# A selective scan with a mixture of experts: the states' sum over n moved from VectorE into TensorE's transposes

## The reference

```python
def step(state, inp):
    ut, dtt, bt, ct = inp
    dA = jnp.exp(jnp.clip(dtt[:, :, None] * A, -5.0, 5.0))
    dB = dtt[:, :, None] * bt[:, None, :] * ut[:, :, None]
    state = dA * state + dB + 1e-06
    y = jnp.sum(state * ct[:, None, :], axis=-1) + D * ut
    return (state, y)
```

## Time and profile before

| | us |
|---|---|
| median of 3 runs | 1398.56 (1398.08 to 1398.73) |
| profiled execution, span | 1397.1 |
| busy: TensorE / VectorE / ScalarE / GpSimd | 1212.7 / 1174.3 / 916.8 / 846.8 |
| weight loads on TensorE, beside its matmuls | 1013.2 |

### The profile page before, as it was taken

How to read it: one execution, slowest core, us unless ns; L and a number is a source line. 1 busy time by engine, 2 the same in 40 slices (tenths; PEclk the granted TensorE clock), 3 DMA queues, 4 the chain that set the end, 5 groups by cost and what they waited for, 6 DMA issues and landing times.

```text
span 1397.1 us, 27129 instructions
## 1 busy us (share of the span) xinstructions
PE 1212.7 (87%) x8709; PEld 1013.2 (73%) x8709; DVE 1174.3 (84%) x2236; ACT 916.8 (66%) x1464; POOL 846.8 (61%) x1370
## 2 busy tenths in 40 slices
PE   6878897899989898998989899898989989898883
PEld 4556666577877777777777778777877878787773
DVE  1699999998898979998898989989798988998423
ACT  4665666577875766777676777668577768772321
POOL 4445445854366864768656783768647684665554
PEclk9899999999999999999999999999999999999997
DMA  6000000032322343143321433232330333256783
GB/s 179 1 1 9 1 9 6 22 125 61 114 82 64 106 136 103 44 128 99 121 67 34 147 97 98 86 111 81 109 120 29 125 92 121 78 184 190 251 271 85
DMA packets 111646, 132.29 MB, mean 95 GB/s; under 512 B 10128, under 2 KB 82704, under 8 KB 111504
## 3 DMA queue, kind: packets, MB, share of 16 engines
q1 hardware_dynamic: 98416, 111.31, 25.7%
q0 software_dynamic: 8192, 16.79, 4.0%
q10 hardware_dynamic: 4896, 2.43, 0.6%
HBM read 102.37 MB, written 28.11 MB: 93 GB/s over the span
## 4 chain that ended last, share of the span: by engine, by line
PE 35%; DVE 31%; ACT 13%; issue 12%; POOL 5%; DMA 2%; DVEq 0%; POOLq 0%; SPq 0%; ACTq 0%
DVE h L1281 14%; DVE yT L1299 11%; PE p_db L1036 5%; PE p_misc L1060 5%; PE p_hT L1053 5%; PE p_dn L1218 4%; PE p_gu L1206 3%; ACT dA L872 3%; ACT L969 2%; POOL ysel L791 2%; ACT hm L969 2%; PE p_gu L1197 2%; PE p_misc L1097 2%; PE p_misc L1141 1%; PE p_misc L1115 1%
## 5 line engine op out<-in xcount | busy, mean ns | idle before, releaser
L1281 DVE TENSOR_TENSOR_SCAN h<-dA,p_db 128x512 f32<-128x512 f32 x512 | 602.4, 1205 | 86.3 <-PE p_db L1036 85.3
L735 POOL TENSOR_SCALAR dBT<-wT,bcT 128x256 f32<-128x256 f32 x704 | 337.1, 479 | 249.2 <-ACT wT L903 140.1
L1299 DVE SCALAR_TENSOR_TENSOR yT<-p_hT,bcT,yT 128x256 f32<-128x256 f32 x960 | 402.2, 472 | 18.0 <-PE p_hT L1053 17.9
L872 ACT ACTIVATE dA<-dt_sb,A_sb 128x510 f32<-128x510 f32 x512 | 330.6, 710 | 26.6 <-DVE h L1281 25.5
L1036 PE MATMUL p_db<-ident,dBT 128*128 128x128 f32 x2048 | 284.4, 277 | 49.4 <-DVE h L1281 44.0
L1053 PE MATMUL p_hT<-ident,h 128*128 128x128 f32 x2048 | 288.9, 279 | 29.8 <-DVE yT L1299 16.6
L1036 PEld LDWEIGHTS p_db<-ident,dBT 128*128 128x128 f32 x2048 | 233.4, 142 | 96.7 <-issue 84.7
L1053 PEld LDWEIGHTS p_hT<-ident,h 128*128 128x128 f32 x2048 | 233.0, 143 | 74.8 <-issue 42.2
L777 POOL DMA_INDIRECT xs_dram<-xn,slot x128 | 127.0, 992 | 90.0 <-ACT dA L872 38.3
L929 ACT ACTIVATE dBT<-wT,eps,bcT 128x256 f32<-128x256 f32 x320 | 163.9, 593 | 0.0
L791 POOL DMA_INDIRECT ysel<-ys_dram,slot x128 | 123.5, 965 | 57.0 <-issue 33.9
(11 more groups left out here) (189 smaller groups left out, 1533.1 us busy)
## 6 DMA issues: line engine op xcount, KB each, us to landing
wring<-w_moe_dram SPq DMA_DIRECT2D x169, 384.0 KB, 4.3
xt<-xs_dram SPq DMA_DIRECT2D x41, 256.0 KB, 5.7
ys_dram<-yo SPq DMA_DIRECT2D x34, 256.0 KB, 2.3
dA<-w_moe_dram SPq DMA_DIRECT2D x16, 384.0 KB, 5.6
x_sb<-x_dram SPq DMA_DIRECT2D x16, 256.0 KB, 4.5
out_dram<-x SPq DMA_DIRECT2D x15, 256.0 KB, 2.5
xs_dram<-ysel SPq DMA_DIRECT2D x4, 512.0 KB, 6.0
xs_dram<-xn,slot POOLq DMA_INDIRECT x128, 2.3
```

The source lines that it names most:

```text
L735: op = pool.tensor_scalar(dBT[:, j % DBT_RING, c], wT[:, g % 2, c], bcT[:, g % 2, c, n:n + 1], STATE_EPS, ALU.mult, ALU.add)
L872: act.activation(dst[:, :, 1:], src[:, :, 1:], ACT.Exp, scale=A_sb[:, half, n:n + 1]).then_inc(exp_done, 1)
L1281: dve.tensor_tensor_scan(h[:, j % 2, half], dA[:, j % DA_RING, half], p_db[half][:], 0.0, ALU.mult, ALU.add).then_inc(scan_done, 1)
L1299: op = dve.scalar_tensor_tensor(yT[:, g % 2, cc], p_hT[pair][:, c], bcT[:, g % 2, cc, NS + n:NS + n + 1], yT[:, g % 2, cc], ALU.mult, ALU.add)
```

## The change

- The scan writes its result over its own input in the PSUM bank p_db. A second VectorE instruction for each half ("t0", "t1") multiplies the bank by C and writes h in SBUF, 128x512. h has three buffers, dA five.
- With channels on partitions, C is a row over tokens, the same in all partitions. So C is transposed once a group ("cT"), copied to c_rows, stored to DRAM by SP ("cs"), and for each unit SP loads its row of 512 numbers spread over all 128 partitions into c_wide ("c", a ring of six, three units ahead).
- TensorE's transposes of h ("h") accumulate over the 16 units of a group in the PSUM pair p_y. VectorE's 60 sums and ScalarE's 4 products a group go. ScalarE copies p_y to yT once a group ("e0", "e1"), and the first unit of the next group waits for that copy.
- A half of p_db is free again when its product with C has ended.
- The orders of all engines are new. DVE_SLOTS, PE_SLOTS and SP_SLOTS are shown; those of ScalarE and GpSimd, and the tables for start and end, are new too. At the end c_wide also holds experts' weights.

```diff
-BY_ACT = 1
-
 COMB_DVE = 4
-DA_RING = 6
+DA_RING = 5
+H_RING = 3
+C_RING = 6
+C_LEAD = 3
 DBT_RING = 3
 DB_LEAD = 2
...
 PE_SLOTS = (
-    "U h N G i0 i1 X", "h U yb0 N i0 i1 yb1 G", "X h U xnT i0 i1 N G", "h u0 N U v0 i0 i1 X X",
-    "N h U G op i0 i1", "U X G h u1 v1 G N i0 i1 h", "U X xn2T G i0 i1 dt0 f0 X",
-    "N h dt1 f1 N U i0 i1 logit X G", "h N U i0 i1 G bc N X", "h U i0 i1", "h G G N X U z0 i0 i1 z1",
-    "h X N U G i0 i1 X U rank", "N h i0 i1", "h G X wT0 U N wT1 G i0 i1 h X N X", "U G N i0 i1 h G",
-    "U i0 i1 X")
+    "h U N yb0 G i0 U i1 h", "N G i0 X G i1 U G U", "yb1 U i0 N h G X xnT h", "i1 u0 i0 N X v0 N i1 op",
+    "i0 h X i1 N u1 G N i0", "X h i1 U U v1 h i0 X", "xn2T G i1 dt0 X f0 h U i0", "dt1 N f1 i1 h logit i0 G N",
+    "X i1 U U i0 X bc N i1", "h G h X i0 G i1 z0 G", "U N N G i0 z1 U cT i1", "U N i0 X G X h rank N",
+    "i1 h X wT0 U i0 wT1 i1 N", "G h G U i0 i1 N h X", "G U X X i0 h i1")
 DVE_SLOTS = (
-    "stats1 s0 s1 y0 P y1", "C Q s0 s1 Q P yd0 y0", "s0 s1 yd1 y1 Q C y0 y1", "s0 C C y0 s1 P y1 P Q",
-    "s0 s1 P y0 y1 x1 C", "stats2 s0 s1 C y0 Q Q P y1", "s0 s1 y0 P y1", "s0 y0 s1 C Q y1 s0 lg P Q",
-    "s1 Q C y0 P C", "s0 y1 s1 r y0 r y1 r P r r s0 r", "Q C s1 r y0 y1 r P r Q r s0 s1 r",
-    "r y0 r P y1 r C C Q r", "s0 r s1 r y0 y1 r r", "C P r r s0 s1 Q r y0 y1 r Q r",
-    "r r C s0 P s1 r r y0 r P y1", "s0 C s1 C Q y0 Q P y1")
+    "C stats1 Q s0 s1 t0 t1 P s0 s1", "Q Q t0 t1 yd0 Q s0 t0 Q s1", "P yd1 P t1 P s0 t0 P s1 t1",
+    "s0 t0 C s1 t1 C x1 C C Q", "s0 t0 s1 C Q stats2 C P t1 s0", "s1 C t0 t1 s0 C t0 P s1 t1",
+    "s0 P t0 s1 t1 lg s0 r t0 s1", "C Q r P r t1 Q s0 Q r", "t0 r s1 Q r C P t1 r s0", "P r r t0 r s1 r t1 s0 r",
+    "P C t0 r C s1 r P r t1", "r s0 r r Q r r r t0 r", "P s1 r t1 Q r s0 r C r", "s1 t0 t1 C P r Q s0 s1 r",
+    "t0 t1 P C r Q Q")
...
 SP_SLOTS = (
-    "", "Y T W W xl Y W", "T", "Y O Y W T", "O W T O O", "T Y T Y W W", "", "Y Y T W T T", "",
-    "T O O O O Y W W", "", "Y Y W O W T T O O W", "", "Y Y W O", "Y T T W W", "T O O Y Y O O T")
+    "W c c O W O", "W Y W W T c", "c T W Y W O", "c Y c O T Y", "T T c Y c c", "O xl W T Y O", "c T Y Y T Y",
+    "T W c O c T", "W W O Y T Y", "W cs c T T O", "O T O Y c Y", "W W O O Y Y", "W c W Y T T", "O O O c")
...
-        h = sb("h", [P, 2, HALVES, TOK])
-        yT = sb("yT", [P, 2, CHUNKS, CH])
-        y_more = sb("y_more", [P, CHUNKS, CH]) if BY_ACT > 1 else None
+        h = sb("h", [P, H_RING, HALVES, TOK])
+        c_wide = sb("c_wide", [P, C_RING, TOK])
+        yT = sb("yT", [P, CHUNKS, CH])
...
-        p_hT = [pb(f"p_hT{i}", [P, 2, CH]) for i in range(PAIRS)]
+        p_y = [pb(f"p_y{i}", [P, 2, CH]) for i in range(PAIRS)]
...
+            def store_rows(g):
+
+                sp.wait_ge(misc_emptied, misc_at["cT", g])
+                at_least(sp, times_c, HALVES * NS * (g - 1))
+                sp.dma_start(row_sets[g % 2].rearrange("n (c t) -> c n t", c=CHUNKS), c_rows[:]).then_inc(rows_stored, 16)
+
+            def load_c(j):
+                if not 0 <= j < UNITS:
+                    return
+
+                g, n = divmod(j, NS)
+                if n == 0:
+                    sp.wait_ge(rows_stored, 16 * (g + 1))
+                at_least(sp, times_c, HALVES * (j - C_RING + 1))
+                sp.dma_start(c_wide[:, j % C_RING], row_sets[g % 2][n:n + 1].broadcast_to([P, TOK])
+                             ).then_inc(c_loaded[j % C_RING], 16)
+
...
+                if name == "cT":
+
+                    at_least(act, rows_stored, 16 * g)
+                    act.activation(c_rows[:], bank[0:CHUNKS * NS, 0:P], ACT.Copy).then_inc(misc_emptied, 1)
...
-            def multiply_state(g, n, pair):
-
-                if g is None:
-                    return
-                j = NS * g + n
-                act.wait_ge(hT_in_psum, PAIRS * j + pair + 1)
-                if n == pair == 0:
-                    act.wait_ge(misc_emptied, misc_at["bc", g])
-                    if g >= 2:
-                        act.wait_ge(misc_in_psum, misc_at["yb1", g - 2])
-                at = (BY_ACT - 1) * g + n - 1
-                if n:
-                    at_least(act, more_added, PAIRS * (at - 1) + pair + 1)
-                for c in range(2):
-                    cc = 2 * pair + c
-                    into = yT[:, g % 2, cc] if n == 0 else y_more[:, cc]
-                    op = act.activation(into, p_hT[pair][:, c], ACT.Copy, scale=bcT[:, g % 2, cc, NS + n:NS + n + 1])
-                op.then_inc(mul_done, 1)
+            def empty_y(g, pair):
+
+                act.wait_ge(y_in_psum, PAIRS * (NS * g + NS - 1) + pair + 1)
+                if pair == 0:
+                    at_least(act, misc_in_psum, misc_at["yb1", g - 1] if g else 0)
+                act.activation(yT[:, 2 * pair:2 * pair + 2], p_y[pair][:], ACT.Copy).then_inc(y_emptied, 1)
...
-                at_least(pe, scan_done, 2 * (j - 1) + half + 1)
+                at_least(pe, times_c, 2 * (j - 1) + half + 1)
...
-            def states_by_token(j):
+            def sum_states(j):
                 if not 0 <= j < UNITS:
                     return
 
-                pe.wait_ge(scan_done, 2 * j + 2)
+                g, n = divmod(j, NS)
+                pe.wait_ge(times_c, HALVES * (j + 1))
                 for pair in range(PAIRS):
-                    if j and (j - 1) % NS < BY_ACT:
-                        pe.wait_ge(mul_done, sums_before(j - 1, pair, True))
-                    elif j:
-                        pe.wait_ge(mac_done, sums_before(j - 1, pair, False))
+                    if n == 0:
+                        at_least(pe, y_emptied, PAIRS * (g - 1) + pair + 1)
                     for c in range(2):
                         for half in range(HALVES):
                             t0 = (2 * pair + c) * P
-                            mm = pe.transpose(p_hT[pair][:, c, half * P:(half + 1) * P],
-                                              h[:, j % 2, half, t0:t0 + P], ident[:])
-                    mm.then_inc(hT_in_psum, 1)
+                            mm = pe.matmul(p_y[pair][:, c, half * P:(half + 1) * P],
+                                           h[:, j % H_RING, half, t0:t0 + P], ident[:], is_transpose=True,
+                                           start=n == c == half == 0, stop=n == NS - 1 and c == half == 1,
+                                           skip_group_check=True)
+                    mm.then_inc(y_in_psum, 1)
...
-                    pe.wait_ge(mac_done, sums_before(NS * g + NS - 1, 1, False))
+                    pe.wait_ge(y_emptied, PAIRS * (g + 1))
                     for c in range(CHUNKS):
                         mm = pe.transpose(bank[:, c * P:(c + 1) * P],
-                                          yT[:, g % 2, c, half * P:(half + 1) * P], ident[:])
+                                          yT[:, c, half * P:(half + 1) * P], ident[:])
...
-                    at_least(dve, hT_in_psum, PAIRS * (j - 1))
                     dve.wait_ge(clamp_done, j + 1)
                 dve.wait_ge(db_by_pe, 2 * j + half + 1)
-                dve.tensor_tensor_scan(h[:, j % 2, half], dA[:, j % DA_RING, half], p_db[half][:], 0.0,
+                dve.tensor_tensor_scan(p_db[half][:], dA[:, j % DA_RING, half], p_db[half][:], 0.0,
                                        ALU.mult, ALU.add).then_inc(scan_done, 1)
 
-            def sum_states(j, pair):
+            def multiply_states(j, half):
                 if not 0 <= j < UNITS:
                     return
 
-                g, n = divmod(j, NS)
-                if n < BY_ACT:
-                    return
-                dve.wait_ge(hT_in_psum, PAIRS * j + pair + 1)
-                if n == BY_ACT == 1:
-                    dve.wait_ge(mul_done, sums_before(j - 1, pair, True))
-                elif n == BY_ACT:
-                    dve.wait_ge(more_added, PAIRS * ((BY_ACT - 1) * (g + 1) - 1) + pair + 1)
-                at_least(dve, mac_done, sums_before(j - 1, pair, False))
-                for c in range(2):
-                    cc = 2 * pair + c
-                    op = dve.scalar_tensor_tensor(yT[:, g % 2, cc], p_hT[pair][:, c],
-                                                  bcT[:, g % 2, cc, NS + n:NS + n + 1],
-                                                  yT[:, g % 2, cc], ALU.mult, ALU.add)
-                op.then_inc(mac_done, 1)
+                dve.wait_ge(scan_done, HALVES * j + half + 1)
+                if half == 0:
+                    at_least(dve, y_in_psum, PAIRS * (j - H_RING + 1))
+                    dve.wait_ge(c_loaded[j % C_RING], 16 * (j // C_RING + 1))
+                dve.tensor_tensor(h[:, j % H_RING, half], p_db[half][:], c_wide[:, j % C_RING], ALU.mult
+                                  ).then_inc(times_c, 1)
```

## The result

The changed kernel takes 1337.03 us (median of 4 runs, 1329.57 to 1340.43), the kernel before 1398.64 in the same rounds: ratio 0.9546, 95% interval 0.9515 to 0.9576. It is 61.6 us faster where 44.6 were forecast. The profiled execution has a span of 1333.1 us, against 1397.1 before.

The account below looks back on a forecast made before the run. TensorE and VectorE, neither full, wait for each other in turns; -3.3 (products) - 0.9 (p_hT) + 1.2 (p_db) = -3.0 us a group, times 15.6 = 46.8, plus 2.5 at the ends: 1354 us, range 1318 to 1410.

Parts of the forecast that it names:

- waits at p_hT: VectorE's wait for the transposes into p_hT, 0.9 us a group, goes.
- Products: VectorE's 32 products with C cost 21.9 us a group, replacing 25.2 of products and sums: a gain of 3.3.
- The scan in PSUM: VectorE's scan writing PSUM instead of SBUF: change taken as 0, up to 0.13 us either way; dearer-scan rival, chance 0.10.
- The handover of p_db: p_db is released only after the product, so VectorE's wait there grows from 5.0 to 6.2 us a group.
- The slower rival: Late p_db refills put scan, product and refill in one ring: +2.5 us a group, 1440 us in all; chance 0.20.
- What TensorE gains: TensorE's 1.6 us a group of waits at p_hT go; summing in PSUM costs nothing; transposing C adds some 0.2.
- larger-gain rival: TensorE's waits at p_misc go too, or PSUM scans are cheaper: 75.6 us a group, 1323 us; chance 0.17.
- C's rows: Loads of C's rows arrive in time, cost nothing; rival: one bare 5 us wait a group, 1432 us, chance 0.05.
- Start and end: First product's store and load cost 2 us at the start; last sums' products, transposes and copies add 0.5 at the end.
- 15.6 equal periods: The 1257 us from first scan to last sums count as 15.6 group periods, each gaining 3.0 us: 46.8 us.

Follow-up runs that it names:

- one_sbuf_input: Changed kernel, but the scan writes its own SBUF buffer and the product multiplies that by p_db, not C's row: ratio 0.956 (1378.7 us, slower chip).
- refills_together: Changed kernel, with TensorE's refill of p_db's half 1 moved right behind that of half 0: 1502.3 us on a slower chip, ratio 1.043.
- no_c_loads: Changed kernel with C's rows loaded only for the first six units, later units reusing them: 1333.0 us, ratio 0.954.
- old_end: Changed kernel with the five tables for the end as in the kernel before, p_y's two copies put ahead on ScalarE: 1324.5 us, ratio 0.947.
- half_product: Changed kernel with only 256 of a half's 512 columns multiplied by C's row: 1309.0 us, ratio 0.936.
- half_turns: Changed kernel with half 1's transposes of h made only in the first unit of a group: 1312.5 us, ratio 0.939.

## Why the prediction was right, and where it wasn't

The direction and the range held; the time was 17 us too high. The closeness is partly luck. The forecast for a group was -3.0 us, and in the even part it is -6.8, more than twice that; what keeps the whole near the forecast is that only ten groups gained so much and the end lost. On VectorE's side the forecast was -3.3 (products), -0.9 (waits at p_hT) and +1.2 (p_db). Measured are -2.5 (all its busy time), -0.9, -1.4 and, at hm, -2.1.

- *Products.* Right: forecast 21.9 us a group, measured 21.4. (In the 21.9 were 0.4 us for overlap that scans lose; the scans' busy time grew by 0.9 us a group, 0.4 of it by their longer duration.)
- *The scan in PSUM.* Right: taken at 0, measured 1217 against 1205 ns, 0.4 us a group. The Trainium skill's 58 and 120 cycles ("VectorE: DVE Perf Modes", errata section), from which I estimated 65 ns for a destination, are for a source in SBUF and in PSUM; for a destination the estimate doesn't come out: the trace has 12, and one_sbuf_input's scans into SBUF took 1212.
- *The handover of p_db.* This is the term that was mis-sized, and its sign with it: forecast +1.2 us a group, measured -1.4. I counted the added chain and gave the new order's parted refills no credit beyond a smaller loss. refills_together shows that much stands on them: 8.4% of the time on its chip. The slower rival (a late refill, 1440 us) was a true mechanism: with the refills side by side it comes, at 1.043 of the kernel before, where I had it at 1.03.
- *What TensorE gains.* p_hT's waits went, as forecast. That the waits at p_misc would go too I had as the larger-gain rival (75.6 us a group); the trace has the largest gone (TensorE's 1.1 us at wT is 0.15), and the group is at 73.8, below that rival's 75.6. It leaves TensorE 2.5 us idle, which I had held against the rival; its busy time, held at 73.4 us, came out at 71.3. VectorE's 2.1 us a group at hm, also gone, was in no term and in no rival; it is the second part of the miss.
- *C's rows.* Right: no wait, and no_c_loads gives 0.3% at most.
- *Start and end.* Forecast +2 and +0.5. The first scan came 0.7 us later. The end became 9.3 longer, which was in no term: I had taken the 106 us behind the last sums as hardly touched, though the change replaces all of its tables. old_end shows 7.6 of it as the tables' work.
- *The early groups.* I took 15.6 equal periods. Three gained nothing, while VectorE's busy time in them fell by 5 us in 284. The granted clock is lower there, 0.95 for 0.98; whether that is the cause wasn't tried. C's loads aren't: from the first x<-p_misc to the fourth no_c_loads takes 217.9 us, the changed kernel 216.3. Less work on either engine shortens them (half_product 208.7, half_turns 209.7).

Had all 15.6 periods gained 6.8 us, the gain would be 106 us. It is 64 of span: 68 from ten groups, 6.5 before the first x<-p_misc, about nothing from the three early and the two last groups, and -9.3 from the end. Why the last two gained nothing stays open.

## What to carry over

When two engines pass a buffer back and forth, the order of their pieces is a part of the data path: the same data path gave 0.955, 1.043, 1.097 and 1.187 of the old time in four orders, so neither can be priced alone. In this kernel it paid to give VectorE's product one of its two inputs in PSUM while GpSimd reads SBUF (1337 against 1412 us). And price the tail's order too, when a change rewrites it.

## What the runs showed that was not expected

- A product of two SBUF inputs is nearly as fast as one with a PSUM input at the median, 691 and 682 ns, but beside GpSimd single ones took up to 3645 ns, and GpSimd's 128x256 scalings up to 1471 ns (518 without such products).
- Writing the scan's result over its own input in PSUM costs 12 ns of 1205.
- Transposes added up over 16 units in the PSUM pair p_y cost no more than plain ones: 273 ns each against 277.
- On two of the four chips the kernel before took 1441.3 and 1438.1 us, 3% more than on the others.
